# A four-stage attention and expert kernel on one core: inputs laid out on the host, first-pass keys and values by four sequences, weight products moved

## The reference, cut to what matters

```python
x = x + xattn0(layernorm(x), ctx, ctx)   # 16 heads of 8; a small network chooses a temperature
x = x + ffn0(layernorm(x))               # rms norm * norm_scale, top 2 of 8 experts, hidden 256
x = x + xattn1(layernorm(x), ctx, ctx)   # 8 heads of 128, dilated windows of 64 keys
x = x + ffn1(layernorm(x))               # top 2 of 8 small experts, hidden 64 each

# the temperature of a sequence and head in xattn0
scores = Q @ K.T / sqrt(8)
feats  = [mean(scores), mean(rowmax(scores)), mean(var(softmax(scores)))]
t      = exp(clip(mlp(feats)))           # 3 -> 64 -> 64 -> 1, gelu
attn   = softmax(Q @ K.T / (2 t))
```

## Time and profile before

| | us |
|---|---|
| median of three runs | 423.61 (423.58 to 423.82) |
| the profiled execution: span, first to last instruction | 446.6 |
| start, up to the first scores | 17.1 |
| pass A, first to last row maximum | 19.1 to 98.8 |
| between the passes, up to the first exponential of pass B | to 120.4 |
| pass B with its routing, up to the first tile | to 218.2 |
| stage C | to 290.7 |
| stages D and E | to 446.6 |

### The profile page before, as it was taken

One profiled execution on the slowest core, in us unless ns is written; L12 is line 12 of the kernel. 1 busy time (PEld: TensorE's weight loads), 2 busy tenths in 40 slices (PEclk: granted clock), 3 DMA queues, 4 the chain that ended last, 5 costly groups with the idle time before them and its releaser, 6 DMA issues.

```text
span 446.6 us, 12483 instructions
## 1 busy us (share of the span) xinstructions
PE 369.6 (83%) x4117; PEld 282.6 (63%) x4117; DVE 314.5 (70%) x1149; ACT 278.5 (62%) x844; POOL 200.6 (45%) x357
## 2 busy tenths in 40 slices
PE   1787876667799999866458999988999999987996
PEld 0433333334556766646458999976788888866786
DVE  3599999996448996865435444447788888876852
ACT  1499999996445664432234888655688778764330
POOL 2654445534014436757583000057787776352200
PEclk9988889985789998999577999998999999996999
DMA  5999899100100000002121333211111000000011
GB/s 113 127 299 285 240 290 263 22 0 1 39 3 6 6 5 26 26 25 64 60 67 49 91 90 95 62 37 41 32 26 26 20 21 15 1 3 1 1 47 49
DMA packets 58498, 29.88 MB, mean 67 GB/s; under 512 B 15811, under 2 KB 56005, under 8 KB 58437
## 3 DMA queue, kind: packets, MB, share of 16 engines
q1 hardware_dynamic: 53652, 23.83, 20.5%
q0 software_dynamic: 2048, 4.20, 3.3%
q10 hardware_dynamic: 2736, 1.07, 1.2%
HBM read 13.82 MB, written 15.27 MB: 65 GB/s over the span
## 4 chain that ended last, share of the span: by engine, by line
PE 55%; DVE 19%; issue 9%; ACT 6%; another core or an unknown queue 3%; POOL 3%; ACTq 2%; DMA 1%; SPq 1%; POOLq 0%; DVEq 0%
PE psum L1886 8%; PE psum L1832 8%; DVE scored L1171 5%; PE psum L1655 5%; DVE negmax L1158 5%; PE psum L1911 5%; PE psum L1897 4%; PE psum L1815 3%; PE psum L1934 3%; PE psum L1950 2%; ACT wa L743 2%; PE psum L2024 2%; ACTq L701 2%; PE psum L1968 2%
## 5 line engine op out<-in xcount | busy, mean ns | idle before, releaser
L743 ACT ACTIVATE wa<-psum,negmax 128x120 f32<-128x120 f32 x256 | 68.7, 454 | 1.2 <-DVE negmax L1158 1.1
L1071 POOL DMA_INDIRECT c_area<-by_expert,rows_at x32 | 31.5, 986 | 68.3 <-DMA by_expert<-c_area 54.5
L1690 PE MATMUL psum<-wa 64*128 64x480 f32 x128 | 41.3, 728 | 10.9 <-issue 7.8
L1171 DVE BATCH_NORM_STATS2 scored<-wa 128x6 f32<-128x240 f32 x128 | 43.3, 400 | 3.8 <-issue 3.5
L960 POOL TENSOR_TENSOR wa<-kT,cst 128x960 f32<-128x960 f32 x16 | 28.7, 1791 | 38.0 <-ACT kT L724 38.0
L1886 PE MATMUL psum<-c_area,work 128*128 128x128 f32 x312 | 45.2, 292 | 0.0
L774 ACT ACTIVATE work<-psum 120x1024 f32<-120x1024 f32 x32 | 31.0, 1022 | 22.3 <-PE psum L1820 22.2
L1514 DVE TENSOR_TENSOR c_area<-psum,c_area 128x256 f32<-128x256 f32 x39 | 16.5, 424 | 38.0 <-ACT c_area L837 25.8
L1886 PEld LDWEIGHTS psum<-c_area,work 128*128 128x128 f32 x312 | 41.8, 208 | 0.1
L1158 DVE TENSOR_REDUCE negmax<-psum 128x8 f32<-128x960 f32 x32 | 36.6, 1145 | 3.1 <-PE psum L1690 3.0
L1031 POOL DMA_INDIRECT by_expert<-scored,rows_at x32 | 32.6, 1018 | 11.5 <-issue 8.3
(11 more groups left out here) (276 smaller groups left out, 983.9 us busy)
## 6 DMA issues: line engine op xcount, KB each, us to landing
by_expert<-work SPq DMA_DIRECT2D x12, 768.0 KB, 6.6
c_area<-by_expert SPq DMA_DIRECT2D x39, 64.0 KB
by_expert<-c_area SPq DMA_DIRECT2D x39, 64.0 KB, 1.6
x<-in_x_dram ACTq DMA_DIRECT2D x16, 64.0 KB, 3.9
work<-in_L_ffn_w_down_dram SPq DMA_DIRECT2D x1, 1024.0 KB
wa<-mscratch SPq DMA_DIRECT2D x64, 2.0 KB
out_dram<-wa SPq DMA_DIRECT2D x32, 32.0 KB, 1.6
wa<-in_ctx_dram SPq DMA_DIRECT2D x16, 60.0 KB, 2.9
```

What stands on the lines that cost most here:

```text
L743: e = nc.scalar.activation(prob[:, z, head, :], psum[:, score_bank(b, half) + h // 4, (h % 4) * LK:(h % 4 + 1) * LK], ACT.Exp, bias=negmax ...
L1071: nc.gpsimd.indirect_dma_start(y_rows[:, r, j, :], None, by_expert[:, :], bass.IndirectOffsetOnAxis(rows_at[:, i:i + 1], 0)).then_inc(ld_y ...
L1171: s = nc.vector.bn_stats(bnout[:, bass.ds(b * HALF0 + h // 2, 1), :].rearrange("p a s -> p (a s)"), prob[:, z, h:h + 2, :].rearrange("p h ...
L1690: m = nc.tensor.matmul(psum[:, score_bank(b, half) + g, 0:4 * LK], qs[rows, z, :], kexp[rows, z, 4 * half:4 * half + 4].rearrange("p i k - ...
```

## The change

The host now prepares every input: x, contexts (turned, and once more in the order of classes for xattn1), `w_up`, `w_down` and Wc turned, weights and constants packed in four arrays. x comes in 4 loads of 256 KB; the output goes out in token classes, one store for each pair.

In pass A the contexts are not turned. Keys of four sequences come from one matmul of 480 columns and one eviction, values of four from four matmuls and one eviction. The product of row sums is replaced by a matmul per sequence (`a_dot`) against masked query sums (`a_mask` on GpSimd). Copies of queries, contexts and maxima on GpSimd go away. Row statistics of all of x are taken before the first norm.

Between the passes, the 12 turned groups go away; the two weight products (`products`, four groups) and the bias sum come there from the end of pass B. `w_up` is no longer multiplied by `norm_scale`; VectorE multiplies the tokens in `ct_turned` instead.

The diff, cut to its core (a line in words stands for several):

```diff
 @block.sync
-  5 loads of ident and nat0; load_ctx(b) for 16 sequences, each after a_tps
-  14 small_loads, 7 large_loads, rconst, 12 clears spread over b = 9 to 15
-  late: window, router1, rb1, ew1, ew2, b1e, 16 of b2rows; expert_rows after mscratch
+  sp.dma_start(first[:, :], t["first"]).then_inc(ld_first, 16)
+  load_ctx(0)
+  sp.wait_ge(ln0_ag, 1)
+  for g in range(1, X_GROUPS): load_ctx(g)
+  smalls, l1N, wcT, rconst  -> ld_heads
+  sp.wait_ge(k_picked, 1)
+  for i in range(NB - 4):
+      if i % 3 == 0:
+          sp.wait_ge(a_xc, 2 + i)
+      clear(i)
+  late, ctxS -> ld_late;  upT, dnT -> ld_w
   sp.wait_ge(temp_dve, T_PARTS)      # then mscratch, load_m as before
-  for c in range(CLASSES): sp.dma_start(out[at:at + 2]..., yacc[class_rows(c), ...])
+  sp.dma_start(out[:, at:at + 2, :], yacc[:, 2 * pair:2 * pair + 2, :])

 @block.scalar
-  load_x(0); bq0, bk0, consts; ... wait ld_first; load_x(1..3)   # 4 loads each
+  for g in range(X_GROUPS):
+      act.dma_start(x[:, SEQS * g:SEQS * (g + 1), :], t["x"][...]).then_inc(ld_x[g], 16)
-  a_project: evict queries (accumulate), keys (accumulate);  a_values: evict values
-  a_turned: copy xc[:, z, :] of LQ + LK columns
-  software_pipeline(act, [(1, a_turned), (3, a_softmax(0)), (3, a_softmax(1)), (1, a_project), (1, a_values)])
+  KEYS_AT = {max(0, SEQS * g - 1): (g,) for g in range(X_GROUPS)}
+  VALUES_AT = {SEQS * g + 2: (g,) for g in range(X_GROUPS)}
+  a_groups(step): evict 480 columns of keys / 512 columns of values where KEYS_AT / VALUES_AT say
+  a_queries: evict queries (accumulate);  a_turned: copy LQ columns
+  software_pipeline(act, [(1, a_turned), (3, a_softmax(0)), (0, a_groups), (3, a_softmax(1)), (1, a_queries)])
-  weight_copies(range(4)) before the small network, (7..11) after it, LATE_GROUPS in pass B
+  copy of the dots; product_copy(0), (1); Gelu table; network; product_copy(2), (3)
   ct_weights(n):
+      if n == 0: act.wait_ge(ld_w, 32)

 @block.gpsimd
-  [(1, a_keep_context), (1, a_expand), (1, a_keep), (3, a_keep_max)]
+  a_mask: qmask = headmask * qsum[b];  a_fold: w1f at b == 6, Wq differences at b == 8..12
+  [(1, a_expand), (2, a_mask), (3, a_fold)]

 @block.vector
-  x_stats(0); copy w4T;  a_norm(2) is followed by x_stats(1..3)
+  for g in range(X_GROUPS): x_stats(g)
-  tensor_tensor(small[:, 5], qsum, ksum); tensor_tensor(small[:, 4], ..., headmask)
-  weight_copies(DVE_GROUPS)
+  after mparts and bias_rows[1]:
+  dve.wait_ge(l1_pe, L1_SUMS); copy bias_rows[0]
+  dve.wait_ge(l1_pe, UVEC);    copy uvec           # was in b_constants, after b_expand(0)
   b_expand ...
   ct_turned:
-      nc.vector.tensor_copy(ct_xT[:, n % 2, :], psum[:, 2, 0:P])
+      nc.vector.tensor_scalar(ct_xT[:, n % 2, :], psum[:, 2, 0:P], nscale, None, ALU.mult)

 @block.tensor
-  turn of nat0; a_turn also turns the context; a_project: three matmuls a sequence
-  [(3, a_scores(0)), (1, a_turn), (3, a_scores(1)), (1, a_project)]
+  a_groups(step): keys: one matmul of 480 columns; values: four matmuls; both wait a_xc >= step
+  a_dot: one matmul of 16 columns
+  [(3, a_scores(0)), (1, a_turn), (3, a_scores(1)), (0, a_groups), (3, a_dot), (1, a_queries)]
-  weights(0..5) first; (6), (7), (8, 9), (10, 11) in the gaps of the network; uvec
+  products(0), products(1) first, after dots_kept
   three matmuls of features; second layer
+  bias of xattn0 (was after the third layer)
   third layer
+  products(2)
   turn of the temperatures
+  products(3); bias sum of xattn1 (18 matmuls, was L1764, L1767); wait l1_dve; uvec (16)
-  late_weights, attention_biases in the last steps of pass B
```

More of the change, by code:

```diff
@@ L200, in build, with of_pack @@
         BANK_KEEP, BANK_TAIL = 7, 6
[L203 to L209, removed]
+        first, smalls, late = (sb(name, [P, widths[name]]) for name in ("first", "small", "late"))
+        def of_pack(name):
+            for pack, whole in (("first", first), ("small", smalls), ("late", late)):
+                if name in cols[pack]:
+                    return whole[:, cols[pack][name]]
+        ident, headmask, halfscale, groupmask, iota, window = (
+            of_pack(n) for n in ("ident", "headmask", "halfscale", "groupmask", "iota", "window"))
         x = sb("x", [P, NB, D])
@@ L1722, in _, with products @@
+            def products(g):
+                _, left, right = product(g)
+                for i in range(4):
+                    m = nc.tensor.matmul(psum[:, g, i * D:(i + 1) * D], left[:, i], right[:, i], start=True, stop=True)
+                m.then_inc(wt_ps, 1)
+            pe.wait_ge(l1_folded, 5)
+            pe.wait_ge(a_q, NB)
+            pe.wait_ge(a_v, X_GROUPS)
+            pe.wait_ge(dots_kept, 1)
+            for g in range(2):
+                products(g)
             pe.wait_ge(a_exp, 2 * NB)
-            pe.wait_ge(w0_sb, 5)
@@ L1745, in _ @@
             m.then_inc(mlp_pe, 1)
-            weights(range(10, C_GROUPS))
+            products(3)
+            nc.tensor.matmul(keep[:, 0:D], ones[0:1, :], bc1, start=True, stop=False)
+            for h in range(H1):
+                m = nc.tensor.matmul(keep[:, 0:D], bqk1[:, 2, h:h + 1].to_broadcast([P, P]), wcT[:, h, :],
+                                     start=False, stop=(h == H1 - 1))
+            m.then_inc(l1_pe, 1)
             pe.wait_ge(l1_dve, 1)
-            pe.wait_ge(l1_folded, 2)
             for h in range(H1):
@@ L2094 @@
         t[name] = nc.dram_tensor(f"in_{name}_dram", a.shape, _mybir.dt.from_np(a.dtype), kind="ExternalInput").ap()
-    out = nc.dram_tensor("out_0_dram", (NB, LQ, D), F32, kind="ExternalOutput").ap()
-    build(nc, cols, t, out)
+    out = nc.dram_tensor("out_0_dram", (P, NB, D), F32, kind="ExternalOutput").ap()
+    build(nc, {n: p.cols for n, p in made.items()}, {n: p.width for n, p in made.items()}, t, out)
     r = _run(nc, [arrays], core_ids=[0])
-    return r.results[0]["out_0_dram"]
+    back = _np.argsort([token_at(p) for p in range(P)])
+    return _np.ascontiguousarray(r.results[0]["out_0_dram"].transpose(1, 0, 2)[:, back, :])
```

583 lines of the change are left out of this document (217 added, 366 removed).

## The result

The changed kernel took 419.57 us, the median of four runs (418.67 to 420.33), beside 423.72 for the kernel before: ratio 0.9897, 95% interval 0.9871 to 0.9923. The forecast was 419.5 in 412.5 to 424.0. The sum is right to 0.1 us, closer than its terms deserve: several of them missed, in opposite ways, so the last tenths are luck.

A forecast was written before the change was run, and what follows sets the result against it. Pass A was taken as bound by ScalarE with VectorE close behind, stage C by TensorE. Terms -1.7 - 1.5 + 2.0 - 1.2 - 1.7 = -4.1 took 423.6 to 419.5 us, range 412.5 to 424.0.

The forecast's parts named there:

- The start: Start to first row maximum: fewer, larger loads and no weight turns bring it from 19.1 to 17.4, -1.7 us.
- The steady pass A: Pass A: ScalarE loses evictions, VectorE then binds; a sequence goes from 5.14 to 5.04 us, -1.5 us.
- 5.14 less the gap of 0.15, 4.99: Pass A: VectorE's floor per sequence in us, its work unchanged, less the one idle gap read in a period.
- Between the passes: Pass A to pass B: products, bias sum and uvec delay the temperatures' expansion and pass B's first scores, +2.0 us.
- The end of pass B: Product matmuls, bias sum and turns leave TensorE's tail, little of it on the path; -1.2 us.
- the 211: Stage C's first tile: its load follows the last scatter, so it cannot come before about 211 us.
- The tail: After the last residual: one store instead of four, and fewer waits of residuals for stores; -1.7 us.
- At nothing: Stage C's multiplication instead of a copy (2.9 us, hidden) and late loads (through at 91 us) cost nothing.
- (a): End of pass B: the remote wait vanishes with the matmuls, -7.2 for -1.2, 413.5 us; chance 0.22.
- (b): Gain eaten: hand-over between passes at +3.7, VectorE's period at 5.14, start at -0.9; about 423.5 us; chance 0.14.
- (c): Pass A: TensorE falls to half clock, a sequence needs 5.6 us; 428 us; chance 0.09.
- (d): Late loads under 113 GB/s hold the temperatures' store on SyncE's queue; 425 us; chance 0.05.

The follow-up runs named there:

- Experiment 2: The changed kernel with GpSimd's first expansion of keys made to wait for the second norm; 418.82 us, ratio 0.9901.
- experiment 4: The changed kernel with two more ScalarE instructions per sequence of pass A, copies into a spare tile; 424.6 us, ratio 1.0024.
- experiment 3: The changed kernel with uvec's 16 matmuls behind pass B's first scores, and VectorE's copies of bias sum and uvec behind its first expansions; 418.18 us, ratio 0.9895.
- experiment 9: The changed kernel with the edits of Experiment 2, experiment 3 and experiment 7, plus four spare matmuls at the end of pass A; 412.27 to 414.16 us, ratio 0.9747.
- Experiment 8: The changed kernel with bias sum and uvec matmuls at the end of pass B, their copies at stage C's first step; 421.26 us, ratio 0.9951.
- experiment 1: The kernel before, unchanged, run again for its second profile (the second profile of before); 424.77 us, span 422.9.
- experiment 7: The changed kernel with the first of the two matmuls of each half of the scores issued twice; 415.76 to 417.34 us, ratio 0.9832.
- experiments 10: The kernel of experiment 9 with the norms of sequences 4 to 15 on GpSimd; 410.07 to 411.97 us, ratio 0.9698.
- 12: The kernel of experiments 10 with a repeated score matmul in one half of the scores only; 413.69 us, ratio 0.9779.
- 11: The kernel of experiments 10 without the repeated score matmuls, spare matmuls kept; 417.39 us, ratio 0.9849.

## Why the prediction was right, step by step

**The start** (-1.7 said, -1.0 and -0.6 measured): right in sign, too large, and for a reason that the sum did not have. DMA moved 287 GB/s from 2 to 6 us, not 203, so x was in before VectorE could use it: its statistics run back to back from 5.54 to 10.33. That this is near the 10.6 of the sum is luck, since VectorE's own 4.8 us set it and not the loads. What was missing was the price of two engines side by side: the norms, taken at 0.3, cost 1.1 and 1.8 beside GpSimd's expansions, which the change makes early enough to meet them. Experiment 2 gives 1.1 of it back.

**The steady pass A** (-1.5 said, -3.5 and -2.2 measured): the mechanism was right, by experiment 4, and the size was off. The step that failed is the floor "5.14 less the gap of 0.15, 4.99", and with it 5.04. One period was read with its single gap, but VectorE's work is the same before and after, and start to start, in the period shown above, it is 0.25 + 2 x (1.07 + 1.27) = 4.93; beside the last three sequences no norm is left to do. Over the pass VectorE had more slack than that one gap: 4.36 us idle from 20 to 95 us in the second profile of before, 1.04 after (third count):

```profile
20.00:95.00 75.00, 57.62 (x226) 24.50 (x226) 70.64 (x182) 74.33 (x315) 39.23 (x72) 0.86 0.79 219
20.00:95.00 75.00, 57.94 (x225) 25.86 (x223) 73.96 (x193) 73.38 (x292) 33.62 (x38) 0.86 0.56 187
```

The earlier trace rows had said so already, 5.9 us idle of 80. The period came to 4.92: without evictions in the way the chain of exponentials, variance and maxima does pack. What the sum left out is the spread: a norm blocked by an expansion, or VectorE behind a stretch of half clock, takes 1.3 to 2 us back in some executions.

**Between the passes** (+2.0 said, +1.5 and +0.8 measured): right as drawn, uvec ahead of the first scores. From the store of the temperatures to the first exponential the changed kernel takes 7.2 and 6.9 us where the second profile of before has 5.3, and experiment 3 brings that to 5.0. Up to the store it is earlier, 11.9 and 11.4 us after the last variance instead of 12.2; the sum had 0.6 for this, the products of row sums and the network without copies beside it, and neither was tested by itself. Products 0 and 1 ran at half clock (3.75 us), which the sum had as a bound, up to 1.7 us dearer. Against before this cost nothing: the last feature's matmuls start 4.9 and 4.7 us after the last variance, 4.8 before, for the weight turns ahead of them were at half clock as well (0.50 in 97 to 104 us). In experiment 9 they start at 3.3, so a faster clock has up to 1.5 to give there.

**The end of pass B** (-1.2 said, -1.2 measured): the number is right by luck, its reasons are not. The sum itself slips: 218.2 less the wait of 6.85 is 211.35, not 212.2, and leaves 0.35 to win over its 211. And the 211 is no bound. Stage C's first loads don't wait for the last scatter: in the second profile of before the first load is issued at 201.9 and the first tile is at 206.8, while scatters go on to 219.7; in the first, too, they went on to 228.3, long after the load at 208.36. "Little of it was on the path" is wrong as well. In the second profile of before the last router matmuls stand behind the bias sum in TensorE's queue, 17.5 us after the last exponential:

```profile
201.80 1.28 PE L1767 MATMUL psum<-work,bqk 128*128 128x128 f32 x10
202.92 0.29 PE L1805 MATMUL psum<-routerT,xnT 128*128 128x8 f32 x2
```

After the change they come 14.5 us after it:

```profile
196.70 0.60 PE L1665 MATMUL psum<-small,xnT 128*128 128x8 f32 x2 [0.46 <-ACT xnT L702]
```

Of these 3.0 us the first silu keeps 1.2; TensorE then waits 3.5 us for VectorE's part of the routing. Experiment 8 agrees: with 34 small matmuls in that queue the last router matmuls come at 18.0 and the first silu 1.6 us later.

**The tail** (-1.7 said): -1.0 behind the last residual, and the residuals of stage E take 19.2 us from first to last instead of 19.6: -1.5. Stages D and E as a whole are no shorter (+0.2 and +0.8 up to the last residual).

**At nothing**: the multiplication is 0.061 longer than the copy and 39 tiles take 56.3 us instead of 57.2; hidden. The late loads are through by 83 us (360 GB/s in 77 to 83, 7 in 83 to 89).

**The rivals.** (a) fell in experiment 1. (b) did not come. (c) is half there: the clock of pass A hardly moved as a mean (0.86; 0.87 in the second profile before), but VectorE has no slack left, so a stretch at half clock costs it 0.65 to 0.71 us where it meets a group of keys and values. The 3.3 us of experiment 7 aren't all the price of this in pass A, which takes 76.4 us with the same edit in experiment 9, and 76.3 and 77.6 without: part lies in stage D, from its first to its last exponential, which takes 90.2 us with the edit (experiment 9), 91.4 and 92.0 without. (d) did not come.

The Trainium skill (TensorE: Matmul & The Clock Gate, the section on the HAM clock gate) lets the clock follow recent activity. The runs agree: the clock of pass A goes from 0.87 with no repeated matmul to 0.98 with one and 1.00 with two.

## What to carry to other kernels

Work taken off the bounding engine is worth what the next engine's queue leaves, counted start to start over a whole period; and once that queue has no gap, every small disturbance of another engine shows in the time. Before an edit on a bound is judged, look whether the bound is steady: the norms on GpSimd gave nothing with stretches of half clock and 2.1 us without, 0.9 of it seen in pass A. Repeated matmuls in a stage where TensorE has room can be worth nearly as much as work saved (3.3 us here beside the change's 4.15), while spare ones in a single wait did not bring the clock back; time many executions before keeping any. And read a prediction's rows from an execution whose span agrees with the timed runs: this one's first profile had waits and stage times that the kernel doesn't have otherwise.

## What the runs showed of the hardware that was not expected

**VectorE and GpSimd block each other on some pairs.** A norm (one input and the output in SBUF) takes 0.33 us alone and 1.81 to 1.83 us beside an expansion of keys (1.79 us); the statistics of x, from 9.08 for 0.84 us, are not slowed by the expansion that starts at 9.50. Which starts first decides: where the norm does, by 0.07 us (28.16 and 28.23 in the first profile of the changed kernel), it takes its 0.33 and the expansion 1.92 instead of 1.79, the longest of this line:

```profile
L844 POOL TENSOR_TENSOR wa<-kT,first x16: 1792/1793/1918, 9.5 to 83.0; 128x960 f32<-128x960 f32 x16
```

The Trainium skill (SBUF — State Buffer, the section on who interferes with whom) has a pair of ports that the two engines share under a lock held for a whole instruction, taken by tensor_scalar from SBUF in its fast mode. The trace agrees, 1.83 against 0.33 us.

**More TensorE work made the kernel faster**: 1.0 us a sequence of repeated matmuls, 3.3 us less time. **An edit in one stage changed the clock of another**: stage D, with the same code, took 90.1, 91.2 and 92.1 us at 1.00, 0.98 and 0.96 (experiments 10, 12 and 11); the way from one to the other was not settled.
